# Routed feed-forward kernel: table numbers loaded into registers four at a time ahead of the tiles, padding DMAs split over two queues

## What is computed

```python
x = x + tanh(g_xattn[0]) * attention(ctx_1024, ctx_1024, layernorm(x), ...)

logits = einsum('bsd,ed->bse', x, gate_w)            # 8 experts
topk_probs, topk_idx = top_k(softmax(logits), 2)
oh = one_hot(topk_idx, 8)
h = gelu(einsum('bsd,fed,bske->bskf', x, w1, oh) + take(b1, topk_idx))   # F = 512
y = einsum('bskf,def,bske->bskd', h, w2, oh) + take(b2, topk_idx)
ffn = sum(y * topk_probs[..., None], axis=-2)

x = x + tanh(g_ffn[0]) * ffn(layernorm(x))
```

## Time and profile before

| | us |
|---|---|
| median of 3 runs | 143.3 (142.46 to 143.58) |
| profiled execution | 142.31 |
| its span | 140.3 |
| PE busy, PEld busy | 84.6, 64.1 |
| DVE, ACT, POOL busy | 73.0, 56.9, 57.8 |

### The profile page before, as it was taken

The page is one execution under the profiler, slowest core; times in us unless marked ns, Lnnn a source line. Parts: engine busy times, 40 slices in busy tenths (PEclk is TensorE's granted clock), DMA queues, the critical chain, the costliest instruction groups (busy, mean ns, idle before and its releaser), DMA issues.

```text
span 140.3 us, 2933 instructions
## 1 busy us (share of the span) xinstructions
PE 84.6 (60%) x823; PEld 64.1 (46%) x823; DVE 73.0 (52%) x255; ACT 56.9 (41%) x114; POOL 57.8 (41%) x80
## 2 busy tenths in 40 slices
PE   6469576566300027005987888878888999993000
PEld 2257355444200011003766677666776888882000
DVE  1589649998839089003954334443344464552043
ACT  3214958975975000000645433355333646550000
POOL 7776022278787710000005333454334554648040
PEclk9968999555555555555599999999999999999655
DMA  4999700011112212105323240000100010000293
GB/s 104 355 428 420 309 0 2 2 43 38 38 59 76 76 37 60 38 2 114 80 58 87 68 98 18 23 13 19 27 19 23 19 32 29 20 23 0 81 257 112
DMA packets 10751, 11.61 MB, mean 83 GB/s; under 512 B 1492, under 2 KB 9704, under 8 KB 10481
## 3 DMA queue, kind: packets, MB, share of 16 engines
q1 hardware_dynamic: 9344, 8.96, 20.1%
q0 software_dynamic: 1248, 2.12, 4.7%
q10 hardware_dynamic: 144, 0.35, 1.1%
HBM read 8.18 MB, written 3.70 MB: 85 GB/s over the span
## 4 chain that ended last, share of the span: by engine, by line
PE 39%; issue 30%; SPq 11%; DMA 8%; POOL 5%; DVE 4%
PE bank L684 7%; PE bank L685 7%; PE bank L671 4%; PE bank L673 4%; SPq L291 4%; PE bank L667 4%; PE bank L672 4%; PE bank L688 3%; SPq L292 3%; PE bank L659 3%; DMA res<-results 3%; DMA wp<-in_wpack 3%; SPq L294 2%; PE bank L681 2%; POOL x_bias L366 2%
## 5 line engine op out<-in xcount | busy, mean ns | idle before, releaser
L388 POOL DMA_INDIRECT results<-y_sb,in_rows x23 | 26.8, 1163 | 53.5 <-DVE y_sb L933 52.9
L508 ACT ACTIVATE hid<-bank 128x512 f32<-128x512 f32 x23 | 13.7, 598 | 51.0 <-PE bank L673 39.7
L933 DVE TENSOR_SCALAR y_sb<-bank,in_rows 128x128 f32<-128x128 f32 x23 | 8.1, 351 | 28.2 <-PE bank L688 28.2
L685 PE MATMUL bank<-w_lo,hid_hi 128*128 x92 | 19.6, 216 | 0.1
L684 PE MATMUL bank<-w_hi,hid_hi 128*128 x92 | 19.4, 216 | 0.1
L673 PE MATMUL bank<-xs_t,w_lo 128*128 128x128 f16 x92 | 18.5, 227 | 0.0
L671 PE MATMUL bank<-xs_t,w_hi 128*128 128x128 f16 x92 | 18.3, 229 | 0.0
L672 PE MATMUL bank<-xs_t,w_hi 128*128 128x128 f16 x92 | 18.3, 227 | 0.0
L320 POOL DMA_INDIRECT dispatched<-rows,slot x16 | 15.8, 990 | 5.1 <-issue 4.5
L928 DVE TENSOR_TENSOR hid_lo<-hid,hid_hi 128x512 f16<-128x512 f32 x23 | 15.7, 682 | 0.2 <-ACT hid_hi L513 0.2
L513 ACT ACTIVATE hid_hi<-hid 128x512 f16<-128x512 f32 x23 | 14.5, 631 | 1.9
(11 more groups left out here) (150 smaller groups left out, 158.8 us busy)
## 6 DMA issues: line engine op xcount, KB each, us to landing
w_sb<-in_w SPq DMA_DIRECT2D x2, 2048.0 KB, 11.3
in_rows<-dispatched SPq DMA_DIRECT2D x23, 65.0 KB, 1.8
res<-results SPq DMA_DIRECT2D x4, 256.0 KB, 3.7
dispatched<-pad_rows SPq DMA_DIRECT2D x9, 65.0 KB, 5.0
ctx_sb<-in_ctx_t SPq DMA_DIRECT2D x1, 512.0 KB, 5.5
out<-out_sb SPq DMA_DIRECT2D x4, 128.0 KB, 1.8
results<-y_sb,in_rows POOLq DMA_INDIRECT x23
wp<-in_wpack ACTq DMA_DIRECT2D x1, 342.0 KB, 3.7
```

Source lines behind the costliest of these rows:

```text
L388: pool.indirect_dma_start(results_dram, bass.IndirectOffsetOnAxis(ap=in_rows[:].bitcast(U32)[:, t, TARGET:TARGET + 1], axis=0), y_sb[:, t, ...
L508: act.activation(hid[:, t % FLAT, :, :], hid_ps[t % HID_PS][:, :].rearrange("p (b s) -> p b s", b=BLOCKS), ACT.Gelu_apprx_tanh, scale=1.0 ...
L685: pe.matmul(to, hid_hi[:, s, b, :], w2_lo[:, bass.ds(e, 1), b * P:(b + 1) * P], start=False, stop=False)
```

## The change

The eight padding DMAs are split: four stay on SP, and four are issued by ACT from its own queue, behind its last weight cast and ahead of its bias copies. In `turn_rows` the wait for `xs_ok` is gone, and in `hidden` the wait for `hid_ok` stands only at tile 3.

```diff
+LOADS = 4
...
+        def table_values(engine, table, largest, t):
+
+            return nc.values_load_multi_w_load_instructions(
+                table[0:1, t:min(t + LOADS, N_TILES)], engines=[engine.engine], min_val=0, max_val=largest,
+                skip_runtime_bounds_check_because="VectorE clamps the table to these bounds")[1]
+
+        def pad_experts(queue, a, b):
+
+            at = nc.values_load_multi_w_load_instructions(
+                pad_from[0:1, a:b], engines=[queue.engine], min_val=0, max_val=PAD_ROW - SLOT_TILE,
+                skip_runtime_bounds_check_because="an expert's count is at most its region's tokens")[1]
+            for e in range(b - a):
+                queue.dma_start(rows_dram[bass.ds(at[e], SLOT_TILE), :], pad_rows[:]).then_inc(filled, 16)
...
             sp.wait_ge(pads_ok, 1)
-            for e in range(EXPERTS):
-                at = sp.value_load(pad_from[0:1, e:e + 1], min_val=0, max_val=PAD_ROW - SLOT_TILE)
-                sp.dma_start(rows_dram[bass.ds(at, SLOT_TILE), :], pad_rows[:]).then_inc(filled, 16)
+            pad_experts(sp, 0, EXPERTS // 2)
             sp.wait_ge(table_ok, 1)
-            first = [sp.value_load(tile_rows[0:1, t:t + 1], min_val=0, max_val=PAD_ROW) for t in range(AHEAD)]
+            first = [at for t in range(0, AHEAD, LOADS) for at in table_values(sp, tile_rows, PAD_ROW, t)]
...
             for t in range(N_TILES):
-                at = first[t] if t < AHEAD else sp.value_load(tile_rows[0:1, t:t + 1], min_val=0, max_val=PAD_ROW)
-                sp.dma_start(in_rows[:, t, :], rows_dram[bass.ds(at, SLOT_TILE), :]).then_inc(loaded[t], 16)
+                if t >= AHEAD and t % LOADS == 0:
+                    first = list(first) + list(table_values(sp, tile_rows, PAD_ROW, t))
+                sp.dma_start(in_rows[:, t, :], rows_dram[bass.ds(first[t], SLOT_TILE), :]).then_inc(loaded[t], 16)
...
+            act.wait_ge(pads_ok, 1)
+            act.wait_ge(pads_set, 1)
+            pad_experts(act, EXPERTS // 2, EXPERTS)
             act.wait_ge(ld_b, 32)
...
                 pe.wait_ge(loaded[t], 16)
-                if t >= 2:
-                    pe.wait_ge(xs_ok, t - 1)
...
-                if t >= HID_PS:
+                if HID_PS <= t < LAG + HID_PS - 1:
                     pe.wait_ge(hid_ok, t - HID_PS + 1)
...
-            experts = [expert_of(t) for t in range(AHEAD)]
             keep_clock(y_ps[0][:, :], CLOCK_ROWS)
+            experts = [e for t in range(0, N_TILES, LOADS) for e in table_values(pe, tile_experts, EXPERTS - 1, t)]
...
                     turn_rows(t + LAG)
-                if t + AHEAD < N_TILES:
-                    experts.append(expert_of(t + AHEAD))
```

More of the change, by code:

```diff
@@ L646, in _ @@
             pe.transpose(b1_bank[:, 0:P], b1_pad[:], ident[:]).then_inc(b1_ps, 1)
-            def expert_of(t):
-                return pe.value_load(tile_experts[0:1, t:t + 1], min_val=0, max_val=EXPERTS - 1)
             def turn_rows(t):
                 pe.wait_ge(loaded[t], 16)
-                if t >= 2:
-                    pe.wait_ge(xs_ok, t - 1)
                 to = xs_ps[t % 2][:, :].bitcast(F16)
```

## The result

| | before | after |
|---|---|---|
| median of 4 runs each, us | 143.41 (142.46 to 143.58) | 121.14 (120.64 to 121.76) |
| profiled execution, us | 142.31 | 120.64 |
| its span, us | 140.3 | 118.6 |
| PE busy, us | 84.6 | 77.3 |

The ratio is 0.8461, with a 95% interval of 0.8406 to 0.8516. The forecast was 121.6, and the profiled execution was to take 120.6.

The account below looks back on a forecast made before the run. SP's issuing before the tiles and PE's sequencer in the tile loop were taken as the bounds. -8.9 - 9.0 - 3.8 = -21.7 from 142.31 gives 120.6 profiled, 121.6 for the median; range 119.6 to 126.0.

Parts of the forecast that it names:

- Part 1, the start: Start of the tiles: hidden(0) moves from 65.34 to 56.4 once SP issues its loads sooner; -8.9 us.
- DVE's program as the floor: Before hidden(0): DVE's weight split from 49.68, biases, a quarter of the second weights, row copy; no start before 56.4.
- SP's 13 instructions: SP's new pad list: 8.8 us at the slow pace, to 50.9; first tile load issued about 53.2, slack 0.8 us.
- PE's six loads: PE's loads of expert numbers ahead of the tiles: at four times the price they would add 0.7 us.
- Part 2, the loads: Tile loop: expert-number loads leave it; twelve iterations go from 2.92 to 2.23 (8.3 us), iteration 2 gives 0.7; -9.0 us.
- Part 3, the waits: PE's tile loop: 38 semaphore instructions on the path go, 0.10 us each; -3.8 us, bounds 0 and -4.6.
- The forecast's own range: Whole time 120.0 to 122.6 us, from the semaphore waits' saving at its upper bound or half its value, and the runs' spread.
- The tiles didn't start later than DVE allows: Rival at hidden(0): slow SP or late pad landing delays the first tile; 122.6 to 125 us, chance 0.22.
- The array didn't hold the loop at 2.2: Rival in the tile loop: array or a data wait holds iterations at 2.2, removed waits give nothing; 125.4 us, chance 0.15.
- The clock rose within the first two iterations: Against the rival that earlier keep_clock leaves the loop at clock 0.50, iterations of 3.5 us; 151 us, chance 0.02.
- The pads' split: Padding DMAs on SP and ACT: four fewer on SP counted as worth four issue slots only.
- The case with 0.56: The main forecast for the whole kernel: 121.6 us, chance 0.56.

Follow-up runs that it names:

- the one-matmul run: Changed kernel with high and low half of the second weights in one tensor, one 256-column matmul replacing each pair in output(): 115.64 us, 0.8075 of the kernel before.

## Why the prediction was right, point by point

**What bounds the kernel.** Right for the chip of the first profile. SP issuing (by the traces of the two kernels there) and PE's sequencer in the loop (by the runs with its instructions put back or taken away) were the two. That the first is not there wherever the kernel runs could not be seen in one trace; what could be seen, and was noted as odd and unexplained, was that a DMA issue took 0.7 us there and 0.33 elsewhere.

**Part 1, the start, -8.9.** Measured -7.9 (65.34 to 57.46) on the first chip, and nothing on a chip whose SP isn't slow. The step that gave DVE's program as the floor is right to 0.2 us: from the start of DVE's split to hidden(0) it is 6.87 us in the trace after, and 56.4 - 49.68 = 6.7 in the sum. Of the missing 1.0, 0.9 is the attention stage, which ran later in that execution. It is lost ahead of 13.7 us, in PE's first matmuls (timeline, before and then after, the same instructions):

```profile
11.76 1.05 PE L538 MATMUL bank<-fused,ctx_sb 128*128 128x128 f32 x8
12.74 0.45 PE L566 MATMUL bank<-ctx_sb,q_t 128*64 128x64 f32 x8
```

```profile
12.30 1.45 PE L555 MATMUL bank<-fused,ctx_sb 128*128 128x128 f32 x8
13.68 0.45 PE L583 MATMUL bank<-ctx_sb,q_t 128*64 128x64 f32 x8
```

Eight of them take 1.45 us where they took 1.05, and the next group, 0.45 in both, is 0.94 us later. That looks like PE on its lower clock for longer; the trace after has no record of the granted clock ahead of 13.1 us, so it is read off the durations alone. It looks like a matter of the execution and not of the change: DVE's split starts at 49.68 and 50.93 in the two traces of the kernel before, and anywhere from 49.46 to 51.80 in eleven of kernels with the change. What decides it stays open; each profiled time carries it in full, and the sum had no term for it.

SP's 13 instructions were to end at 50.9 at the slow pace; the last pad goes out at 49.6, and tile 0's load is issued at 52.6, not at 53.2. ACT, for which I had allowed the same slow pace, doesn't have it. PE's six loads were put behind `keep_clock` in time as in program; they started at 46.9, beside its matmuls, so their price could not matter.

**Part 2, the loads, -9.0.** Right: 8.17 us for twelve by the run with the loads put back, 0.68 each against 0.69. hidden(0) to hidden(3) got 1.3 us shorter where 0.7 had been counted for the one load there.

**Part 3, the waits, -3.8.** The mechanism was right and the size was low: 4.6 us for 37 waits, 0.125 per wait and not 0.10. The bound that I had set above (0.12) was the value, or just below it. The reasoning that chose less than the upper end had no row for it.

**The sum** came out to 0.5 us since -7.9 - 1.3 - 12.8 + 0.2 = -21.8 (-21.7 before rounding): hidden(3) to (22) gave 12.8 (50.65 to 37.86) in place of 12.0, the iterations ahead of it 0.5 more than counted, and the tail is 0.2 longer. That these offset the missing 1.0 of the start, and the profiled execution came out at the very 120.6, is luck: the start alone moved by up to 2.3 us from one trace to the next.

**The range.** The forecast's own range, 120.0 to 122.6, doesn't follow from its reasons: part 3 at half its value adds 1.9 us and gives 123.5. The measured 121.1 lies in it either way.

**The rivals.** The tiles didn't start later than DVE allows: 2.4 us of slack were left (54.56 to 56.99), three times what was forecast. The array didn't hold the loop at 2.2, nor at 1.99; it takes over at 1.76 in the one-matmul run, which has 128 columns more an iteration than the 1.7 that the sum of 27 short matmuls and the bias gave. The clock rose within the first two iterations, as before: the window from hidden(0) to hidden(2) has a granted clock of 0.54, the next one 1.00. `keep_clock` alone had raised it earlier, for a stretch in which PE had nothing to do (`keep_clock` itself ran from 46.85 to 50.42 at 0.50), and from 54.56 to hidden(0) it was back at 0.50:

```profile
50.66:54.07 3.41, 0.00 (x0) 0.00 (x0) 3.41 (x4) 0.00 (x0) 0.00 (x0) 1.00 0.15 41
```

The Trainium skill gives some 200 ns per register ("Runtime: NRT & Kernel Launch", Instruction fetch mechanics). The page has that figure for loads from HBM (the DRAM beside the chip), and these read SBUF: here three registers more take 0.08 us more, 0.380 against 0.303.

**The pads' split.** The prediction weighed it by a rule of the Trainium skill ("Trainium Kernel Development and Optimization", Key Constraints), that issuing from several engines saves only issue time. The runs agree with it: where SP runs at full pace the split saves 2 us of issue time that nobody waits for, and the two kernels with the pads on one queue took 120.7 and 120.5 us, no more than the changed one. Where SP is slow, ACT issued its half in 1.9 us. Whether the kernel would be slower there without the split was not run.

**The chances.** The case with 0.56 came in. What was not among the rivals is that the size of the gain depends on the chip, or on whatever sets its level: 22.3 us where SP is slow, 13.2 us where it isn't. The time after is 121 us on both, since DVE sets the start in either; a forecast given as a gain, not as a time, would have been wrong on the second.

## What to carry to other kernels

Where matmuls are short and picked by registers, count what PE's sequencer has to do between them: a semaphore wait that never waits cost 0.125 us, a checked register load 0.68, and putting two matmuls with their register instructions into one of 256 columns took an iteration from 1.99 to 1.76, the array's own time. When a stretch of a queue shows every kind of instruction at one and the same strange duration, take the kernel's profile on a second chip before you price a change by it. Before work is moved to an idle engine, look whether the two can run side by side at all: DVE's and POOL's passes over 128x1024 numbers did not.

## What the runs showed of the hardware that I had not expected

- The kernel before has two levels, 134.2 to 134.3 us on three chips and 143.4 to 143.6 in two other comparisons, while the changed kernel took 121 on one chip of either kind. In all three traces from the slow kind SP's instructions take 0.7 us each for a stretch in which POOL issues indirect DMAs, whatever the instruction, and DVE waits twice for 1.3 to 2.1 us ahead of the pads; ACT's DMA issues in the same stretch, in the two traces that have them, take their usual time. What it is that these chips do differently stays open.
- DVE's 128x1024 operations and POOL's work hold each other up. Beside them sends of 0.96 us took up to 1.97 (but one took 0.96), while DVE lost nothing; and two POOL subtractions of 2.1 us each kept DVE's first operation, started 0.02 us behind them, for 5.28 us in place of 1.2.
- From the start of DVE's split to hidden(0) it is 6.87 us in every one of the ten traces in which hidden(0) waits for DVE's copy and DVE's split is as in the changed kernel, while the start itself wanders over 2.3 us.
- A TENSOR_LOAD of four numbers takes 0.380 us on PE, one of a single number 0.303.
